# Which queue brings the windows, and how many rows SP fetches: a graph layer with eight gathers less on GpSimd

## The reference

```
h  = relu(layernorm(x))                          # 6250 x 64
p1 = tanh(h @ pp_W1 + pp_b1) @ pp_W2 + pp_b2
t  = concat(p1[src], p1[dst]) @ pi_W1 + pi_b1    # per edge
t  = (t @ pi_W2 + pi_b2) @ pi_W3                 # 64 x 8 per edge
i1 = einsum("ecb,eb->ec", t.reshape(E, 64, 8), edge_attr)
i1 = tanh(i1 @ ii_W1 + ii_b1) @ ii_W2 + ii_b2
out = x + segment_sum(i1, dst, 6250)
```

## Time and profile before

| what | value |
|---|---|
| time of the profiled execution | 1972.48 us |
| its span, first to last instruction | 1970.7 us |
| median of three runs | 1965.04 us |
| TensorE busy (matmul) | 1717.0 us, 87% |
| GpSimd busy | 1474.1 us, 75% |
| VectorE busy | 1453.4 us, 74% |
| ScalarE busy | 1109.4 us, 56% |
| mean granted TensorE clock | 0.969 of full speed |
| gathers of u rows, L573 | 1416 to the ring and 100 before |
| row transfers of SP, L443 | 2560 |

### The profile page before, as it was taken

How to read it: one execution, slowest core, us unless ns; L and a number is a source line. 1 busy time by engine, 2 the same in 40 slices (tenths; PEclk the granted TensorE clock), 3 DMA queues, 4 the chain that set the end, 5 groups by cost and what they waited for, 6 DMA issues and landing times.

```text
span 1970.7 us, 61801 instructions
## 1 busy us (share of the span) xinstructions
PE 1717.0 (87%) x20012; PEld 1125.7 (57%) x20012; DVE 1453.4 (74%) x1937; ACT 1109.4 (56%) x2419; POOL 1474.1 (75%) x1561
## 2 busy tenths in 40 slices
PE   7699999998888888888888888888888988888998
PEld 6366666665555555555555555555555555555666
DVE  7688778787777777777776777777767767777776
ACT  5666666565555555555555555555555655555554
POOL 7777777777777777777777777777777777777774
PEclk8799999999999999999999999999999999999999
DMA  6543333333333333333323333333333333333332
GB/s 139 123 80 64 67 65 60 65 71 65 58 61 60 58 62 58 66 63 57 62 56 61 62 61 66 62 55 61 57 63 64 60 63 62 57 58 55 57 76 47
DMA packets 271300, 128.56 MB, mean 65 GB/s; under 512 B 192747, under 2 KB 243546, under 8 KB 270959
## 3 DMA queue, kind: packets, MB, share of 16 engines
q0 software_dynamic: 49408, 50.69, 16.5%
q10 hardware_dynamic: 55738, 50.10, 10.6%
q1 hardware_dynamic: 165938, 25.50, 7.9%
HBM read 119.48 MB, written 6.00 MB: 64 GB/s over the span
## 4 chain that ended last, share of the span: by engine, by line
POOL 55%; issue 21%; PE 11%; SPq 9%; DMA 1%; ACT 1%; DVE 0%; ACTq 0%; POOLq 0%; DVEq 0%
POOL u_rows L573 55%; SPq L443 6%; PE bank L1388 4%; SPq L440 2%; PE bank L1371 1%; PE bank L1483 1%; SPq L482 1%; PE bank L1395 1%; PE spread_ps L1380 1%; PE bank L1355 1%; DMA p<-L_gnn_pi_W 0%; DMA v_win<-v_tab 0%; PE spread_ps L1217 0%; DMA u_rows<-u_tab,src_e 0%; PE bank L1223 0%
## 5 line engine op out<-in xcount | busy, mean ns | idle before, releaser
L573 POOL DMA_INDIRECT u_rows<-u_tab,src_e x1416 | 1348.0, 952 | 432.0 <-issue 430.7
L996 DVE TENSOR_TENSOR o_sb<-st_sb,spread_ps 128x2048 f32<-128x2048 f32 x391 | 893.6, 2286 | 403.0 <-PE spread_ps L1380 370.3
L761 ACT ACTIVATE st_sb<-bank,s_bias 64x256 f32<-64x256 f32 x1564 | 734.2, 469 | 452.9 <-PE bank L1371 431.3
L1388 PE MATMUL bank<-o_sb,g_sb 128*64 128x256 f32 x6256 | 792.4, 397 | 1.0 <-DVE o_sb L996 0.8
L1388 PEld LDWEIGHTS bank<-o_sb,g_sb 128*64 128x64 f32 x6256 | 427.3, 140 | 225.2 <-issue 23.9
L1371 PE MATMUL bank<-ident,u_rows 128*128 128x128 f32 x1436 | 257.5, 302 | 196.7 <-DMA u_rows<-u_tab,src_e 195.9
L1060 DVE TENSOR_TENSOR hot_t<-loc_bc,bank 126x512 bf16<-126x512 bf16 x391 | 268.6, 687 | 90.6 <-PE bank L1483 44.8
L1371 PEld LDWEIGHTS bank<-ident,u_rows 128*128 128x128 f32 x1436 | 188.7, 191 | 247.5 <-DMA u_rows<-u_tab,src_e 237.8
L1483 PEld LDWEIGHTS bank<-hot,t_sb 128*65 128x65 f32 x3128 | 215.0, 139 | 148.9 <-issue 146.9
L749 ACT ACTIVATE tt_sb<-bank,z_bias 128x256 f32<-128x256 f32 x391 | 185.5, 474 | 157.1 <-PE bank L1388 157.1
L752 ACT COPY t_sb<-bank 128x256 f32<-128x256 f32 x391 | 146.6, 375 | 213.6 <-PE bank L1395 205.1
(11 more groups left out here) (147 smaller groups left out, 350.7 us busy)
## 6 DMA issues: line engine op xcount, KB each, us to landing
loc_bc<-loc_tab ACTq DMA_DIRECT2D x387, 126.0 KB
sp_stage<-u_tab SPq DMA_DIRECT2D x2560, 0.2 KB
u_rows<-u_tab,src_e POOLq DMA_INDIRECT x1416
v_win<-v_tab SPq DMA_DIRECT2D x391, 15.8 KB
basis<-edge_attr SPq DMA_DIRECT2D x24, 256.0 KB
v_tab<-acc_all SPq DMA_DIRECT2D x6, 336.0 KB
basis<-u_tab,src_e POOLq DMA_INDIRECT x100, 2.9
u_tab<-basis SPq DMA_DIRECT2D x6, 224.0 KB
```

Source lines behind the costliest of these rows:

```text
L573: pool.indirect_dma_start(out=u_rows[:, g % UR, j, :] if g >= AHEAD else first_u[:, g - XG, j, :], out_offset=None, in_=u_tab[:, :], in_of ...
L761: last = nc.scalar.activation(tiles[h * D:(h + 1) * D, j], s_ps[part].rearrange("p (q a e) -> p q a e", q=2, a=TILES), ACT.Identity, bias= ...
L996: return nc.vector.tensor_tensor(o_sb[:, r, :, :].rearrange("p c (j e) -> p j c e", j=TILES), st_sb[:, r, :].rearrange("p (j e) -> p j e", ...
L1388: last = nc.tensor.matmul(z_ps[h * D:(h + 1) * D, 0:2 * P], g_sb[:, c, :], o_sb[:, r, c, 2 * h * P:(2 * h + 2) * P], start=(c == 0), stop= ...
```

## The change

- SP's loop no longer loads the starts of windows nor issues the windows. A new function on ScalarE, `load_v`, does both, the first four windows ahead of its loop, and that of group n+4 after `make_t(n - 2)` in step n. It waits once for `base_read` and for a new semaphore `tables_in`, which SP raises when the tables have landed.
- SP fetches seven groups, 60, 112, 164, 216, 268, 320 and 372, each beginning 59 steps before its own (step 1, 53, ...), with ROWS = 10 a step, and AT_ONCE = 16 numbers with one load. 512 rows take 52 steps, so one group follows the other without a gap. GpSimd leaves these seven out.
- Two groups share a semaphore of `first_u_in`; TensorE waits for both.

```diff
-    ROWS = 7
-    BY_SP = [(83, 4), (157, 78), (231, 152), (305, 226), (380, 300)]
-    AT_ONCE = 8
+    ROWS = 10
+    BY_SP = [(52 * k + 60, 52 * k + 1) for k in range(7)]
+    AT_ONCE = 16
...
+        tables_in = sem("tables_in")
-        first_u_in = sems("first_u_in", AHEAD - XG)
+        first_u_in = sems("first_u_in", (AHEAD - XG + 1) // 2)
...
                 v_landed()
+                sp.sem_inc(tables_in, 1)
                 load_sp_idx()
                 at = None
                 for g in range(NG):
-                    if g % 8 == 0:
-                        _, starts = nc.values_load_multi_w_load_instructions(
-                            base_row[0:1, g:min(g + 8, NG)], engines=[mybir.EngineType.SP], min_val=0, max_val=N - W,
-                            skip_runtime_bounds_check_because="VectorE made them from dst and cut them at N - W")
-                    start = starts[g % 8]
                     if g >= VR:
                         sp.wait_ge(s_ready, g - VR + 1)
-                    sp.dma_start(v_win[:, g % VR, :], v_tab[bass.ds(start, W), :, :].rearrange("n w d -> (n w) d")
-                                 ).then_inc(v_in[g % VR], 16)
...
-                        ).then_inc(u_in[g % UR] if g >= AHEAD else first_u_in[g - XG], 16)
+                        ).then_inc(u_in[g % UR] if g >= AHEAD else first_u_in[(g - XG) // 2], 16)
...
+            def load_v(g, starts):
+
+                if g % 8 == 0:
+                    _, starts = nc.values_load_multi_w_load_instructions(
+                        base_row[0:1, g:min(g + 8, NG)], engines=[mybir.EngineType.Activation], min_val=0,
+                        max_val=N - W,
+                        skip_runtime_bounds_check_because="VectorE made them from dst and cut them at N - W")
+                if g >= VR:
+                    act.wait_ge(s_ready, g - VR + 1)
+                act.dma_start(v_win[:, g % VR, :], v_tab[bass.ds(starts[g % 8], W), :, :].rearrange("n w d -> (n w) d")
+                              ).then_inc(v_in[g % VR], 16)
+                return starts
...
                 tanh_rows(len(UNITS) - 1)
+                act.wait_ge(base_read, 1)
+                act.wait_ge(tables_in, 1)
+                starts = None
+                for g in range(VR):
+                    starts = load_v(g, starts)
...
                     if has(n - 2):
                         make_t(n - 2)
+                    if has(n + VR):
+                        starts = load_v(n + VR, starts)
...
-                        pe.wait_ge(first_u_in[g - XG], 64)
+                        pe.wait_ge(first_u_in[(g - XG) // 2], 64 * min(2, AHEAD - XG - (g - XG) // 2 * 2))
```

## The result

The changed kernel takes 2022.43 us (median of 4 runs, 2019.13 to 2027.46) against 1965.38 before: a ratio of 1.029 (95% interval 1.0277 to 1.0302), 57 us slower. The forecast was 2024.

What follows compares the result with a forecast made beforehand. GpSimd's gathers bound the kernel before, SP's issuing after: first placing 354.3 plus five rounds of 268.2, then 4.9, 310.1 and 19.5 give span 2029.8, less 5.7 is 2024 us; range 1985 to 2106.

Steps and rivals of the forecast that it cites:

- The mechanism: SP, issuing its row transfers and number loads, falls behind GpSimd by 12.1 us a round; TensorE and GpSimd wait.
- SP's round: SP from placing one fetched group to the next, 52 steps and 512 rows: 268.2 us against GpSimd's 256.1.
- Placing: SP issuing the copy of a fetched group: 1.10 us, 1.3 with its surroundings, once a round.
- The pieces: SP's transfers of src and basis pieces: 3.55 us each, 3.2 a round, 11.4 us.
- The waits that now stand alone at each step: SP's wait that stood with the window issue: taken as 0.02 us a step, 1.0 us a round.
- the two slopes: Two per-number prices, 0.044 and 0.068 us, for SP's load of sixteen (d): 1.14 or 1.33 us; 1.22 taken.
- The first placing: SP places group 60 at 354.3 us, its rows starting at about 65; GpSimd is let on at 359.2.
- less than 256.1, no new stall: SP's sixth round has only 472 rows and takes 248.4 us, under GpSimd's 256.1, so no stall is added.
- the end: After group 320, GpSimd let on at 1700.2 us, 310.1 us of gathers, then 19.5 to the end: span 2029.8.
- rival 2: SP's load of sixteen is two of eight, 1.68 us: round 281.2, time 2105 us; chance 0.12.
- rival 3: Load of sixteen (d) between 0.88 and 0.93 us, gains and stalls cancel: 1961 to 1969 us; chance 0.05.
- Rival 1: SP keeps up and the change pays, for a load of sixteen (d) below 0.89 us: time 1952; chance 0.13.

Runs made afterwards that it cites:

- that half alone: Changed kernel with SP's fetches as before (five groups, 7 rows a step, loads of eight), windows and starts on ScalarE: 1967.52 us, 1.0008 of before.
- the kernel without pieces: Changed kernel with the pieces of src and edge_attr issued by ScalarE instead of SP, loads of sixteen: 1960.59 us, 0.9961 of before.
- SP's half alone: Kernel before with seven groups, ten rows a step, loads of sixteen and paired semaphores, SP keeping starts and windows: 2277.87 us, 1.159 of before.

## Why the prediction was right, and where it wasn't

*The mechanism held.* SP hardly waits between its first row and its last copy (the profile puts 10.6 us of waits for TensorE at its loads, in 14 pieces of at most 1.2 us, most of which is the load's own time, as said above); its round, not GpSimd's, sets the pace; TensorE waits for each copy, 27.0 us at group 60, 34.4 to 35.7 at the next five and 12.6 at the last (expected 25 to 30 at each); GpSimd stood 9.2 us at group 60 (expected 14), and 6.7 to 10.6 in the later rounds (expected 12). One expected sign did not show: SP's lines were to have five sixths of the chain and have 15%, because the chain leaves SP at its loads. That the windows' move is free on ScalarE: shown by that half alone.

*The terms of SP's round.* Predicted 268.2, with the measured load of 1.227 in its formula 268.5; measured 264.9. Three terms were 3.6 us too large together. Placing took 349.93 to 350.68, 0.75 us, not 1.3. The pieces: taken off SP they gave 264.9 - 255.7 = 9.2 us a round, 2.9 us each, not 3.55. The waits that now stand alone at each step, put at 1.0 us a round, cost nothing: the row behind a wait starts 0.41 us after the row before it, as a row without one does (medians over the five rounds). And rows 211.2, loads 32 x (1.227 + 0.057) = 41.1, leftovers 2.5 and placing 0.75 make 255.6, while the kernel without pieces has 255.7. One slip goes the other way: the middle of the two slopes' 1.14 and 1.33 is 1.235, not 1.22, which would have made the time some 3 us longer.

*The first placing* came at 349.9, not 354.3: SP's first load starts at 61.8 us, so its rows start near 63 and not 65, and the terms above were too large here too. The copy landed in 2.0 us, not in the 4.1 of the earlier trace rows.

*The step that failed* is "less than 256.1, no new stall", and the end built on it. It looked at GpSimd alone. It held for GpSimd, which did not stand there. But in the sixth round TensorE stood before the copy of group 372 for 12.6 us, with GpSimd ahead of it, and behind it TensorE had 18 groups left at its own pace. The timeline of TensorE and GpSimd at the end, which answers to the earlier trace rows:

```profile
1918.49 1.22 PE L1386 MATMUL bank<-ident,u_rows 128*128 128x128 f32 x4 [12.56 <-DMA u_rows<-sp_stage]
...
1925.30 0.71 PE L1386 MATMUL bank<-ident,u_rows 128*128 128x128 f32 x4
...
2003.70 0.71 PE L1386 MATMUL bank<-ident,u_rows 128*128 128x128 f32 x4
```

From group 372 to group 390 it took 85.2 us, 4.73 a group, and 16.0 from there to the end of the span. The last gather had started at 1988.9 us, 314.6 us behind the copy of group 320, where the sum has 315.0; but the span ended 30.8 us behind it and not 19.5. So the end hangs on SP's last copy: 1916.4 + 103.3 = 2019.7. From the copy of group 320 to the end it was 345.4 us, not the 334.5 of 4.9 + 310.1 + 19.5.

*How near the number was.* In the span the first placing (-4.4), five rounds (5 x -3.3) and the end (+10.9) leave the prediction 10.1 us too high. The step from span to time was 8.4 us the other way: I took 5.7 off, because the profiled execution before was 7 us over its median, and here the median is 2.7 over the span. That profiled execution was a long one; the half with ScalarE alone had 1966.4 against 1967.5. The error of the mechanism is thus 10 us, not 2, and these 10 are themselves 20.9 us too many up to the fifth round and 10.9 too few at the end. That they cancel is luck.

*The rivals.* One instruction loads the sixteen (224 lines L441), so rival 2 falls, and with a load of 1.227 us so does rival 3, which wanted 0.88 to 0.93. Rival 1's threshold, d below 0.89, wasn't reached in the load, but its other side was: 9 us a round saved elsewhere on SP's queue makes the same kernel faster than before.

The Trainium skill's sentence that issuing from several engines saves only sequencer time ("DMA: Bandwidth & Descriptors", Issuing engines are not separate DMA queues) agrees with these runs. The page calls that time usually small beside the transfer; in this kernel it is what counts: the sequencer time of SP is the bound, and taking the windows and their loads from it, about 0.6 us a step, is worth 2278 - 2022 = 255 us.

## What to carry to other kernels

An issuing queue is an engine with a budget. Before giving it more, add up its instructions for one round (each row, load, copy and the side jobs) from a stretch in which it never waits, and compare with the round of the engine it relieves; here 264.9 against 256 made a saving of 10 us a loss of 57, and 255.7 made it a gain of 7 or 8.

When a queue runs late, everything behind it in its order is late, also small things that nobody thinks of, as the last group's inputs here. And check the end for each engine by itself: the last hand-over may bind an engine that was never the bound before.

## What the hardware showed unexpectedly

A load of numbers into SP's registers costs 0.34 us and 0.056 us for each number, up to 32 in one instruction.

A wait that is already met costs SP nothing that can be measured: from row to row 0.41 us in the median, with a wait between them and without.

After a stall TensorE starts at the lower of its two clock levels, 1.2 and not 2.4 GHz. In the stage table (length, busy us of PE, PEld, DVE, ACT, POOL, granted clock, DMA share, GB/s) the granted clock is 0.50 in the 3 us behind the first hole, where TensorE is busy throughout; it is 0.75 in a stretch that holds the second hole, and 0.86 in the next, which still begins at the lower level:

```profile
352.00:355.00 3.00, 2.99 (x26) 2.05 (x28) 1.07 (x1) 1.69 (x4) 1.19 (x2) 0.50 0.09 23
560.00:612.00 52.00, 17.81 (x214) 11.53 (x213) 15.98 (x22) 11.67 (x26) 38.28 (x41) 0.75 0.20 40
612.00:640.00 28.00, 24.03 (x278) 15.88 (x280) 17.86 (x22) 14.03 (x31) 16.98 (x18) 0.86 0.35 63
```

The first four products of L1386 after a hole took 1.22 us instead of 0.71, the sixteen of L1403 behind them 2.9 to 3.7 instead of 1.95, and the next group came 5.8 to 6.9 us later instead of 4.1 to 4.5. At the first six holes that costs a second short wait of GpSimd, 1.14 us at group 69, and nothing more, since SP's round sets the pace. Behind the last hole TensorE's own pace sets the end, and some 2.5 us of the 10.9 that the prediction lacked there are this slow start (6.81 us to the next group).

The copy of 128 KB landed in 2.0 us in the changed kernel and in 4.1 us before (medians). It isn't TensorE's waiting that makes it fast: with SP's half alone, where TensorE didn't wait for it, it took 2.0 to 2.9 us. In the changed kernel the DMA engines were 20% busy in the 2 us behind each of the first three copies, before 39% to 100% in the 4 us behind each of the first four; whether that is the cause wasn't tried.
